# The late expert table between VectorE's large operations, record scatters one step earlier, and a stage end without GpSimd's drain

## The reference

```python
x = x + tanh(g_xattn) * attention(layernorm(x), ctx, ctx)
xt = layernorm(x).reshape(4096, 256)
logits = einsum('td,ed->te', xt, gate_w)              # 8 experts
w_topk, sel = top_k(logits, 2)
w_topk = softmax(w_topk)
combine = zeros((T, E)).at[arange(T)[:, None], sel].add(w_topk)
h = silu(einsum('td,edf->tef', xt, w1))               # 256 -> 1024
y = einsum('tef,efd->ted', h, w2)                     # 1024 -> 256
x = x + tanh(g_ffn) * einsum('ted,te->td', y, combine)
```

## Time and profile before

| what | us |
|---|---|
| median of three runs | 764.19 |
| the three runs | 774.77, 764.18, 764.19 |
| profiled execution, its own time | 762.03 |
| span of its profile | 760.3 |
| TensorE busy | 728.7 (96% of the span) |
| VectorE busy | 584.4 (77%) |
| ScalarE busy | 377.3 (50%) |
| GpSimd busy | 371.3 (49%) |

### The profile page before, as it was taken

How to read it: one execution, slowest core, us unless ns; L and a number is a source line. 1 busy time by engine, 2 the same in 40 slices (tenths; PEclk the granted TensorE clock), 3 DMA queues, 4 the chain that set the end, 5 groups by cost and what they waited for, 6 DMA issues and landing times.

```text
span 760.3 us, 23505 instructions
## 1 busy us (share of the span) xinstructions
PE 728.7 (96%) x7980; PEld 605.1 (80%) x7981; DVE 584.4 (77%) x1270; ACT 377.3 (50%) x671; POOL 371.3 (49%) x308
## 2 busy tenths in 40 slices
PE   7999999999999999998899999999999999999994
PEld 6567777767677776666789988899999999999994
DVE  5788879798897989796778868767767676767761
ACT  3686676777677667754344422233333333333331
POOL 5135445766676766674424647433343433334332
PEclk9999999999999999999999999999999999999998
DMA  8452443536282725433888875433334333333422
GB/s 302 152 153 98 153 153 131 175 132 216 72 284 77 250 85 197 130 121 111 248 219 215 233 203 103 67 49 48 52 45 55 43 54 48 49 53 45 57 33 26
DMA packets 93177, 93.88 MB, mean 123 GB/s; under 512 B 59312, under 2 KB 77936, under 8 KB 92720
## 3 DMA queue, kind: packets, MB, share of 16 engines
q1 hardware_dynamic: 31184, 64.97, 25.3%
q0 software_dynamic: 13392, 18.03, 13.7%
q10 hardware_dynamic: 48528, 9.92, 7.5%
HBM read 53.89 MB, written 37.95 MB: 121 GB/s over the span
## 4 chain that ended last, share of the span: by engine, by line
PE 39%; DMA 7%; issue 3%; POOL 2%; ACTq 1%; ACT 0%; DVE 0%; POOLq 0%; DVEq 0%
PE h_ps L1483 20%; PE pair_ps L1496 18%; DMA out<-y,meta 7%; POOL records L1742 1%; POOL out L1736 1%; ACTq L158 0%; ACT y L1555 0%; ACTq L160 0%; POOLq L141 0%; PE h_ps L1527 0%; DVE bx_l L1614 0%; POOL last_rstd L1748 0%; ACT bx_h L1543 0%; DVE ht_h L1626 0%; DVE w_now L1620 0%
## 5 line engine op out<-in xcount | busy, mean ns | idle before, releaser
L1736 POOL DMA_INDIRECT out<-y,meta x71 | 132.6, 1868 | 222.5 <-ACT y L1555 191.0
L1483 PE MATMUL h_ps<-bx_h,w_now 128*128 128x128 f16 x2272 | 194.5, 219 | 5.9 <-DVE bx_l L1614 4.5
L1496 PE MATMUL pair_ps<-weights,ht_h 128*128 x1136 | 190.7, 273 | 1.8 <-issue 1.2
L1483 PEld LDWEIGHTS h_ps<-bx_h,w_now 128*128 128x128 f16 x2272 | 152.4, 98 | 11.2 <-DVE bx_l L1614 6.5
L1483 PE MATMUL h_ps<-bx_l,w_now 128*128 128x128 f16 x1136 | 156.2, 219 | 0.5 <-issue 0.5
L1496 PE MATMUL pair_ps<-weights,ht_l 128*128 x568 | 154.8, 273 | 0.0
L1496 PEld LDWEIGHTS pair_ps<-weights,ht_h 128*128 128x128 f16 x1136 | 110.2, 97 | 17.1 <-issue 2.6
L1555 ACT ACTIVATE y<-pair_ps,meta 128x256 f32<-128x256 f32 x71 | 33.7, 474 | 169.3 <-DVE meta L1609 85.2
L1626 DVE CAST ht_h<-hid 128x1024 f16<-128x1024 f32 x71 | 49.7, 700 | 80.9 <-ACT hid L1548 79.7
L1306 POOL TENSOR_TENSOR r_l<-r,r_h 128x512 f16<-128x512 f32 x62 | 75.3, 1214 | 73.7 <-ACT r_h L832 71.8
L1548 ACT ACTIVATE hid<-h_ps 128x1024 f32<-128x1024 f32 x71 | 72.6, 1022 | 63.9 <-PE h_ps L1483 63.1
(11 more groups left out here) (250 smaller groups left out, 1236.5 us busy)
## 6 DMA issues: line engine op xcount, KB each, us to landing
stage<-in_w SPq DMA_DIRECT2D x16, 1024.0 KB
w_split<-split SPq DMA_DIRECT2D x14, 1024.0 KB, 6.5
weights<-w_split SPq DMA_DIRECT2D x14, 1024.0 KB
rows<-records ACTq DMA_DIRECT2D x268, 32.0 KB
xin<-in_x SPq DMA_DIRECT2D x7, 512.0 KB, 5.5
x_even<-in_x SPq DMA_DIRECT2D x4, 512.0 KB
x_odd<-in_x SPq DMA_DIRECT2D x4, 512.0 KB
out<-x_even SPq DMA_DIRECT2D x4, 512.0 KB
```

What stands on the lines that cost most here:

```text
L1483: last = nc.tensor.matmul(h_ps[r % 2][:, c, :], w1_now[:, r % 2, s, k * F + c * P:k * F + c * P + P], xt[:, r % 2, k, :], start=(j == 0 an ...
L1496: last = nc.tensor.matmul(y_ps[r % 2], ht[:, r % 2, c, :], weights_at(e, s, WN // 2 + c * D, D).rearrange("p o n -> p (o n)"), start=(c == ...
L1736: pool.indirect_dma_start(out, bass.IndirectOffsetOnAxis(meta[:, r, 0:1].bitcast(U32), 0), y[:, r % 2, :], None, compute_op=ALU.add).then_ ...
```

## The change

Three edits, all in the expert stage.

First, the 18 operations of the late table with the numbers 2 to 19 (19 is a pair) are no longer issued in three pieces behind `step`. `between(i, gap)` is called five times in VectorE's step, after `turn_x`, `take_w1`, `x_low`, `split_h` and `copy_meta`, and in the steps of blocks 15 to 18 (`LATE_AT` is 15) each call issues one operation: 2 to 6 in step 15, 7 to 11 in step 16, 12 to 16 in step 17 and 17 to 19 in step 18. The wait for the operation before now stands ahead of an operation and no longer behind it. The operations are the same.

Second, GpSimd scatters a job's records in routing steps 6 to 9, which is behind the adds of blocks 7 to 10 and 13 to 16.

Third, the block is opened with `no_gpsimd_drain=True`: its end does not drain GpSimd and uses a barrier of semaphores alone.

```diff
+    LATE_AT = 8 + BEHIND + 1
...
-    block = ctx.enter_context(nc.Block())
+    block = ctx.enter_context(nc.Block(no_gpsimd_drain=True))
...
             if there(i + 1):
                 e = expert_of(dve, i + 1)
                 turn_x(i + 1, (r + 1) % RB)
+                between(i, 0)
                 take_w1(i + 1, (r + 1) % RB, e)
+                between(i, 1)
                 x_low(i + 1, (r + 1) % RB)
+                between(i, 2)
...
             split_h(i, r)
+            between(i, 3)
             if there(i + 1):
                 copy_meta(i + 1, (r + 1) % RB)
+            between(i, 4)
...
-            if j == 1 and i >= 8:
-                late_table(i)

         def late_table(i):

+            dve.wait_ge(table_ops, i - 1)
+            if i == 2:
+                op = nc.vector.tensor_tensor(under[:, :, :], carry.steps_128[:, :, :], count1[:, :].unsqueeze(2).broadcast_to([1, E, T // P]), ALU.is_lt)
...
-                link(nc.vector.tensor_tensor(cum[:, :, :], carry.upto[:, :, :], left[:, :].unsqueeze(1).broadcast_to([1, E, E]), ALU.mult), 8)
-                link(nc.vector.tensor_reduce(ends[:, :], cum[:, :, :], AX.X, ALU.add), 9)
...
+            if i == 19:
                 nc.vector.tensor_scalar(table[:, NB + SAFE:2 * NB], blk_s[:, :], float(E * REGION), None, ALU.min)
-                nc.vector.tensor_scalar(table[:, SAFE:NB], blk_e[:, :], float(E - 1), None, ALU.min).then_inc(table_ops, 1)
+                op = nc.vector.tensor_scalar(table[:, SAFE:NB], blk_e[:, :], float(E - 1), None, ALU.min)
+            op.then_inc(table_ops, 1)
+
+        def between(i, gap):
+
+            if isinstance(i, int) and LATE_AT <= i < LATE_AT + 4:
+                op = 2 + 5 * (i - LATE_AT) + gap
+                if op <= TABLE:
+                    late_table(op)
...
-            if i in (7, 8, 9, 10):
-                if i == 7:
+            if i in (6, 7, 8, 9):
+                if i == 6:
                     pool.wait_ge(routed.slots_done, j + 1)
                     pool.wait_ge(rec_done, j + 1)
-                for n in range(2 * (i - 7), 2 * (i - 6)):
+                for n in range(2 * (i - 6), 2 * (i - 5)):
                     scatter(rec[j], slot[j], n, records_in)
```

More of the change, by code:

```diff
@@ L1640, in step @@
             split_h(i, r)
+            between(i, 3)
             if there(i + 1):
                 copy_meta(i + 1, (r + 1) % RB)
+            between(i, 4)
         nc.vector.memset(loads_base[:, :], 0.0).then_inc(loads, 1)
         take_w1(0, 0, carry.first_expert)
-        def link(ins, i):
-            ins.then_inc(table_ops, 1)
-            dve.wait_ge(table_ops, i)
         def routing(j, i):
@@ L1688, in routing @@
                 row_numbers(nc, dve, route, routed, carry, j, slot[j])
-            if j == 1 and i >= 8:
-                late_table(i)
         def late_table(i):
-            if i == 8:
[L1695 to L1703, removed]
@@ L1704, in late_table @@
-            if i == 9:
-                link(nc.vector.tensor_tensor(cum[:, :, :], carry.upto[:, :, :], left[:, :].unsqueeze(1).broadcast_to([1, E, E]), ALU.mult), 8)
-                link(nc.vector.tensor_reduce(ends[:, :], cum[:, :, :], AX.X, ALU.add), 9)
[L1709 to L1713, removed]
@@ L1714, in late_table @@
-            if i == 10:
[L1716 to L1720, removed]
-                nc.vector.tensor_scalar(table[:, NB + SAFE:2 * NB], blk_s[:, :], float(E * REGION), None, ALU.min)
-                nc.vector.tensor_scalar(table[:, SAFE:NB], blk_e[:, :], float(E - 1), None, ALU.min).then_inc(table_ops, 1)
+            dve.wait_ge(table_ops, i - 1)
@@ new lines, in late_table @@
+            if i == 2:
+                op = nc.vector.tensor_tensor(under[:, :, :], carry.steps_128[:, :, :], count1[:, :].unsqueeze(2).broadcast_to([1, E, T // P]), ALU.is_lt)
+            if i == 3:
+                op = nc.vector.tensor_reduce(blocks[:, :], under[:, :, :], AX.X, ALU.add)
+            if i == 4:
+                op = nc.vector.tensor_tensor(taken[:, :], carry.full[:, :], carry.full_ends[:, :], ALU.subtract)
+            if i == 5:
+                op = nc.vector.tensor_scalar(taken[:, :], taken[:, :], float(SAFE), 0.0, ALU.add, ALU.max)
@@ new lines, in late_table @@
+            if i == 6:
+                op = nc.vector.tensor_tensor(taken[:, :], taken[:, :], carry.full[:, :], ALU.min)
+            if i == 7:
+                op = nc.vector.tensor_tensor(left[:, :], blocks[:, :], taken[:, :], ALU.subtract)
+            if i == 8:
+                op = nc.vector.tensor_tensor(cum[:, :, :], carry.upto[:, :, :], left[:, :].unsqueeze(1).broadcast_to([1, E, E]), ALU.mult)
+            if i == 9:
+                op = nc.vector.tensor_reduce(ends[:, :], cum[:, :, :], AX.X, ALU.add)
@@ new lines, in late_table @@
+            if i == 10:
+                op = nc.vector.tensor_copy(jump[:, :], blocks[:, :])
+            if i == 11:
+                op = nc.vector.tensor_tensor(jump[:, 0:E - 1], blocks[:, 0:E - 1], taken[:, 1:E], ALU.subtract)
+            if i == 12:
+                op = nc.vector.tensor_tensor(past[:, :, :], carry.block_no[:, 0:LATE, :], ends[:, :].unsqueeze(1).broadcast_to([1, LATE, E]), ALU.is_ge)
+            if i == 13:
+                op = nc.vector.tensor_reduce(blk_e[:, :], past[:, :, :], AX.X, ALU.add)
@@ new lines, in late_table @@
+            if i == 14:
+                op = nc.vector.tensor_tensor(past[:, :, :], past[:, :, :], jump[:, :].unsqueeze(1).broadcast_to([1, LATE, E]), ALU.mult)
+            if i == 15:
+                op = nc.vector.tensor_reduce(blk_s[:, :], past[:, :, :], AX.X, ALU.add)
+            if i == 16:
+                op = nc.vector.scalar_tensor_tensor(blk_s[:, :], carry.block_no[:, 0:LATE, 0], taken[:, 0:1], blk_s[:, :], ALU.add, ALU.subtract)
+            if i == 17:
+                op = nc.vector.tensor_scalar(blk_s[:, :], blk_s[:, :], float(P), None, ALU.mult)
@@ new lines, in late_table @@
+            if i == 18:
+                op = nc.vector.scalar_tensor_tensor(blk_s[:, :], blk_e[:, :], float(REGION), blk_s[:, :], ALU.mult, ALU.add)
+            if i == 19:
+                nc.vector.tensor_scalar(table[:, NB + SAFE:2 * NB], blk_s[:, :], float(E * REGION), None, ALU.min)
+                op = nc.vector.tensor_scalar(table[:, SAFE:NB], blk_e[:, :], float(E - 1), None, ALU.min)
[5 more added lines that the diff above has]
+                    late_table(op)
```

## The result

The changed kernel takes 759.58 us, the median of 22 runs (756.46 to 766.13), against 764.25 us of the kernel before in the same session (22 runs, 761.65 to 774.77): a ratio of 0.9931 with an interval of 0.9915 to 0.9947, which is 5.3 us (4.1 to 6.5) of 764 (the two medians by themselves lie 4.7 apart). In a later group one execution of the changed kernel was disturbed, 1737 us, and is left out. The profiled execution took 760.15 us with a span of 758.4. Of the 7.2 us that I had summed up some 5 came, and the traces have to say what is missing.

What follows compares the result with a forecast made beforehand. TensorE was taken as the bound, full after 482 us with 5.0 us idle before; 3.6 us there plus 3.6 us for the drain, 7.2 in all, gave 757.0 us from a median of 764.19; range 754.0 to 761.8.

Steps and rivals of the forecast that it cites:

- the 7.2 us: Whole kernel: total gain, 3.6 us for TensorE up to block 21 plus 3.6 us at the program's end.
- The drain: Program's end: GpSimd's drain is a fixed cost of about 3.7 us; without it the gain is 3.6 us.
- Rival A: Program's end: what follows the kernel may wait for GpSimd just as long; time 760.6 us, chance 0.12.
- D: Expert stage: slots come late for the first job and GpSimd stands; 760.6 plus up to 3, 763 us; chance 0.06.
- The late table: VectorE's steps 15 to 18: with late operations between big ones they last 20.7 instead of 22.6 us in all.
- rival C: VectorE's steps 15 to 18: each of the 18 waits stops the sequencer 0.79 us; time 767.7 us, chance 0.05.
- the 1.9 us counted for the links: VectorE's late table operations: 17 links between small operations cost 0.11 us each, 1.9 us, which the new order saves.
- The records: GpSimd's scatters a block earlier: last one near 471, ScalarE's 3.54 us wait before block 21 goes.
- Block 21: TensorE starts this block at 477.8, where it was 481.4: gain 3.6 us, with ends of 0.5 and 5.9.
- The step that failed: TensorE after 482 us: full for 265 us, so nothing but its own work counts there.
- the middle: TensorE's stretch before block 21, 437 to 482 us: the new order of late operations and scatters gains 3.6 us.
- Rival B: After 441 us: GpSimd's serial adds, not VectorE, set the steps and the middle gives nothing; 760.6 us, chance 0.14.

Runs made afterwards that it cites:

- the swap: Changed kernel with VectorE's weight copy behind `x_low` instead of ahead of it in the steps of blocks 64 to 69: 757.46 us, 0.9929; again 760.28 us, 0.9949.

## Why the prediction was right, and where it was wrong

**The drain: right.** 3.6 us was the term; alone it measured 4.4 (2.8 to 5.9). Rival A is out: the time less the span is 1.75 us, as it was 1.73, so nothing behind the kernel pays the drain again. That the change doesn't do what it says (D) is out as well: no add or scatter near 413 us waits for the slots.

**The late table: right within 0.4 us a step.** VectorE's `bx` rows of the changed kernel, with the late operations in the third step:

```profile
447.47 0.45 DVE L165 STREAM_TRANSPOSE bx<-rows 128x256 f32<-128x256 f32 x1 [0.59 <-issue]
...
452.92 0.45 DVE L165 STREAM_TRANSPOSE bx<-rows 128x256 f32<-128x256 f32 x1 [0.72 <-issue]
453.29 0.11 DVE L1705 TENSOR_TENSOR late_left<-late_blocks,late_taken 1x8 f32<-1x8 f32 x1
453.33 1.21 DVE L1621 COPY w_now<-weights 128x4096 f16 x1
...
457.88 0.45 DVE L165 STREAM_TRANSPOSE bx<-rows 128x256 f32<-128x256 f32 x1 [0.62 <-issue]
458.25 0.42 DVE L1715 TENSOR_TENSOR late_past<-block_no,late_ends 1x304 f32<-1x304 f32 x1
458.60 1.21 DVE L1621 COPY w_now<-weights 128x4096 f16 x1
459.73 0.45 DVE L1717 TENSOR_REDUCE late_blk_e<-late_past 1x38 f32<-1x304 f32 x1
...
463.91 0.45 DVE L165 STREAM_TRANSPOSE bx<-rows 128x256 f32<-128x256 f32 x1 [0.48 <-issue]
...
468.74 0.44 DVE L165 STREAM_TRANSPOSE bx<-rows 128x256 f32<-128x256 f32 x1
```

The steps lasted 5.45, 4.96, 6.03 and 4.83 us; 5.35, 4.93, 6.05 and 4.4 were predicted. The last one was 0.4 longer because `ht_h` waited 0.41 us for ScalarE's `hid`. From the end of the operation of gap 3 to the next `bx` it took 0.91, 0.81 and 0.78 us, where 0.79 was counted. No late operation has an idle time ahead of it, so rival C, which needed 0.6 us a wait, is out. The four steps took 21.3 us where 20.7 were predicted and 22.6 measured before, so the 1.9 us counted for the links were there to be saved; behind 453.29 the next operation, a large one that waits for nothing, starts 0.04 us later, where the linked ones stood 0.19 apart.

**The records: right for TensorE.** In the changed kernel the last scatter starts at 471.99 (predicted: near 471), and ScalarE's wait of 3.54 us is gone:

```profile
475.16 0.48 ACT L1556 ACTIVATE y<-pair_ps,meta 128x256 f32<-128x256 f32 x1 [2.85 <-PE pair_ps L1497]
475.54 0.40 ACT L1544 CAST bx_h<-bx 128x256 f16<-128x256 f32 x1
```

In the second profile of the changed kernel the last scatter starts at 473.23 and 2.17 us of that wait remain, without harm there: block 21 begins at 477.5. In the third it starts at 474.13, and no such wait stands there.

**Block 21: 479.0, 477.5 and 481.1 in the three profiles; predicted 477.8.** The gain is 2.4, 3.9 and 0.3 us for the 3.6 predicted. Block 16 came at 450.1, 450.4 and 452.1 (predicted 451.2). From block 17 on TensorE was to run at 5.32 a block; in the first profile it didn't, for it stood in blocks 19 and 20 three times for some 0.5 us, for a reason that no view names (two of the three rows):

```profile
469.53 0.22 PE L1484 MATMUL h_ps<-bx_l,w_now 128*128 128x128 f16 x1 [0.51 <-issue]
470.25 0.38 PE L1497 MATMUL pair_ps<-weights,ht_h 128*128 x2 [0.51 <-issue]
```

Such gaps stand there in the first and third profile of the changed kernel, in the one with the first job's records back and in the second of the swap, and in none of the ten others; in those four, blocks 19 and 20 together took 12.6 to 12.9 us, 2.0 to 2.3 more than two blocks of 5.32, and the cause stays open.

**The step that failed** is in the first paragraph: "behind it nothing but TensorE's own work counts". I read the 265 us behind 482 us as TensorE's because it was full there. It is still nearly full (264.42), and yet the end is not its own: the chain of serial adds had kept pace by only a little. What counts is whether the last add is on time, and that hung on the very wait that the change takes away. Worked out on the two profiles: TensorE's last matmul is 2.35 us earlier; the last `y`, held by the landing of an add, is only 1.52 us earlier; the last add goes from 1.68 to 5.01 us behind it, another 3.33 us lost, which makes 1.81 us later; with the drain's 3.7 us less the span is 1.9 us shorter, as read. In the medians, 5.3 us less the 4.4 of the drain alone leaves 0.9 for the middle, which the measurement can't tell from nothing, where the sum had 3.6. So the time lies in the range by the drain, and because the range reached up to the rivals; the term for the middle is not borne out. Rival B priced the middle at nothing too, but its sign is absent in the first profile (the two waits of `meta` for adds, 2.6 us, end at 440.27 and 445.56, in steps 13 and 14, and none lies in steps 15 to 19), and its mechanism, adds that set VectorE's steps at the late table, isn't what happened: those steps shortened as planned, and the gain was lost at the program's far end.

The prediction could have seen it: in the earlier trace rows the adds of 413 to 433 us stand 6 to 7 us apart, more than TensorE's 5.32, so GpSimd falls behind there, and it needs spare time in some later place. I priced that delay only where it touches `meta`, and never asked where it is caught up.

The spread between executions is as large as what is sought: the changed kernel's 22 runs go from 756.5 to 766.1 us, along with the mean granted clock (correlation -0.73, about 0.7 us for each 0.001). That slope is no more than lost clock costs by itself, 0.001 of 760 us. Part of the mean is the tail and costs nothing: in the first profile the clock is 0.50 from 752 us to the end, behind TensorE's last matmul at 748.20. The rest are stretches of about 3 us at 0.50, at 12 to 16 us in six of the fourteen profiles, at 370 in two, and at the two holes named above. The spread is why the drain alone, the swap and the changed kernel can't be ranked here.

## What to carry to other kernels

When a wait on the way of the bounding engine goes, look for who used it: a serial chain whose period is near that engine's catches up only in such waits, and without them it carries its delay to the end of the program, where it shows in full. A full engine over the last third of a span doesn't prove that it sets the end; compare the lag of each consumer behind its producer, block by block. In such a chain the lag is worth more than a time from one profile: it came out the same in every profile of a version, where TensorE's times moved by up to 3.6 us. And price the fixed costs at the end by themselves: one line about a drain gave most of what a careful new order gave.

## What the hardware showed that I had not expected

The issue of an indirect DMA on GpSimd depends on what VectorE does: 1.55 us with nothing in the way; if a 1.2 us `w_now` copy or a `ht_l` operation already runs, it ends 1.43 us behind the end of that operation (39 and 40 adds, within 0.02 us); if the copy starts within the issue, it ends 0.08 to 0.14 us behind the end of the copy (40 adds of the changed kernel). An add that starts at most 0.03 us after `ht_l` isn't held (1.55, four adds of the two swap profiles), and then `ht_l` takes 1.27 to 1.29 us instead of 1.23. Nor is one held by an `ht_l` that starts 0.85 or 0.97 us into it (1.55, two adds of the same profiles). The Trainium skill describes this in "SBUF — State Buffer", section "SBUF: two separate sides": VectorE and GpSimd contend for one port pair by an exclusive lock that is held for the whole instruction, taken also by a VectorE operation with two inputs in that memory, this one only against a GpSimd instruction that reads it. The runs agree in the main: both kinds of operation hold an add, and an add reads its rows' numbers there. They don't agree where the add takes hold first: `ht_l` beside an issue of 1.55 us lasts only some 0.05 us longer.

So adds come in two phases of VectorE's step: those in time meet the `w_now` copy and take 1.90 us, those a block late meet `ht_l` and the copy too and take 2.35. Being late costs 0.45 us more a block; with the 5.3 us that such a period comes to, it keeps itself up.

A drain of GpSimd costs 3.6 to 3.7 us with nothing left to drain: its end moved with SyncE's, 760.1 less 756.4 before, and 762.6 less 759.0 with the records alone.
